# Attention's value product taken in blocks of three 512-query score chunks instead of one key tile

## The chip, the cores and the metric

The kernel runs on one core of one Trainium2 chip. The metric is the device time of one execution in microseconds (us); smaller is better.

## What is computed

The reference is one transformer block over two sequences of 2048 tokens with 256 channels: a layer norm with modulation, attention with 16 heads of 16 channels, a gated residual, and then a mixture of eight experts. Only the attention matters here; cut to it, for each of the 32 pairs of sequence and head:

```python
scores = jnp.einsum('bhqd,bhkd->bhqk', q, k) / jnp.sqrt(jnp.float32(Hd))   # 2048 x 2048 per head, Hd = 16
attn = jax.nn.softmax(scores, axis=-1)
out = jnp.einsum('bhqk,bhkd->bhqd', attn, v)
out = out.transpose(0, 2, 1, 3).reshape(B, T, D)
return out @ W_o + b_o
```

All operands are float32. The weights are scaled so that the scores are large, so the row maxima are subtracted before the exponential.

## The kernel before

The program is a row of stages: modulation and norm, projection of q, k and v, attention, output projection with the second norm, and the experts. The change touches attention (lines 487 to 766), and only the counts of some waits in the stage after it.

Attention works on 64 units. A unit is one head and one half of its queries (1024 queries, two chunks of 512), against 16 tiles of 128 keys; one unit is 16 steps, one per key tile, and there are 1024 steps. Each step has three kinds of TensorE work.

- `fill_group` (L724) computes scores with queries on the partitions, for 128 queries and 1024 keys, as two matmuls of 512 columns. The group lies in one of two slots of two PSUM banks. VectorE reduces it to row maxima (L695). This work is done 24 steps (`AHEAD`) before the step that needs the maxima. After a unit's 16 groups VectorE joins the maxima (L701) and turns them (L707); GpSimd splits them in two parts (L616, L618), and DMAs of SyncE's queue put them beside the q operand (L540, L545).
- `scores` (L737) computes the same scores with keys on the partitions, 128 keys by 512 queries, with the maxima subtracted by extra rows of the contraction. There is one matmul for each half of the queries; each fills one of three PSUM banks (`SCORE_BANKS`). Chunk n is half n % 2 of step n // 2. ScalarE turns each chunk into probabilities in `pt` (L677, the exponential), which has six slots of one step. Chunk n may be computed when the exponential of chunk n - 3 has ended.
- `weigh` (L749) multiplies the probabilities with the values and a column of ones. The 1024 queries are four strips of 256, each on its own 32 columns of the array and its own 32 partitions of bank 7. Operands are float32, and the program has two instructions for each call, so a step has eight weight loads and eight matmuls. I call the four that run side by side a stage: a step's `weigh` is two stages of 256 columns.

The array stands in two layouts. `fill_group` and `scores` contract over 48 and 50 rows, and use rows 0 to 63 for one half and rows 64 to 127 for the other: two such matmuls, one in each row half, can run together. I call such a pair, or a lone one, a slot. `weigh` uses all 128 rows and a quarter of the columns. So a step goes from one layout to the other and back once.

The order on TensorE is written out by hand. Step s runs `weigh(s - 3)`, `scores(s, 0)`, `fill_group(s + 24)`, `scores(s, 1)`; once in a unit, where a new unit's first tile is weighed, the first two change places, so that ScalarE has time to copy the finished unit out of bank 7 (`take_output`, L667). SyncE's queue stores this copy, loads it back turned to the layout of the output projection (L563) and loads the sums of the exponentials in four pieces (L569); later VectorE inverts the sums (L510), they go out and come back by DMA (L515, L518), and GpSimd normalises (L523).

Of the kernel before, what the change touches and what calls it, by code (L numbers as in the profile page):

```python
# [20 lines left out]
HD = D // H  # L21
# [27 lines left out]
QT = TH // P  # L49
LEAD = 8  # L50
AHEAD = KT + LEAD
LAG = 3
PTS = 6
HG = D // HD // KD
BITS = 7
# [27 lines left out]
def adaln_moe_block(nc, x, w_q, b_q, w_k, b_k, w_v, b_v, w_o, b_o, w_s, router_w, router_b,  # L83
                    w1, b1, w2, b2, c, w_mod, out):
    ctx = ExitStack()
    with ctx:
# [400 lines left out]
        with nc.Block() as block:  # L487
# [15 lines left out]

            acc = bank(7)[:, 0:STRIP]

            def group_slot(n):
                return bank(3 + 2 * (n % 2), 2)

# [17 lines left out]
            def _(sp):  # L526
# [30 lines left out]
                def load_output(u):  # L557
                    g, f = divmod(u, HALVES)
                    rows = slice((g % HG) * HD, (g % HG + 1) * HD)
                    cols = slice(f * TH, (f + 1) * TH)  # L560
                    strips = o_dram[u].rearrange("(j r) c -> r j c", r=32)
                    sp.wait_ge(o_stored[u % 2], (u // 2 + 1) * 16)
                    sp.dma_start(ao[rows, g // HG, cols].rearrange("r (j c) -> r j c", c=STRIP),  # L563
                                 strips[0:HD]).then_inc(o_in[f], 16)
                    if g >= HG:
                        sp.wait_ge(inverse_saved, ((g // HG - 1) * HALVES + f + 1) * 16)
                    for j in range(4):
                        at = (g % HG) * HD + 4 * j
                        sp.dma_start(sums_c[at:at + 4, f, :],  # L569
                                     strips[HD, j].rearrange("(q c) -> q c", q=4)).then_inc(sums_in[f], 16)  # L570

                def finish_group(u):
                    h, f = divmod(u, HALVES)
# [26 lines left out]
            def _(pool):  # L600
# [2 lines left out]
                                          v_all[:, (h // H) * KT:(h // H + 1) * KT, (h % H) * HD:(h % H + 1) * HD]).then_inc(v_staged, 1)  # L603

                def restage_v(h):
                    pool.wait_ge(pv_done, (h - NBUF + 1) * HALVES * KT)
                    stage_v(h, h % NBUF)

                g = nc.gpsimd
# [8 lines left out]
                    g.tensor_tensor(low, rowmax_t[:], high, ALU.subtract).then_inc(parts_made, 1)  # L618

                def normalise_part(k, f):  # L620
                    pool.wait_ge(o_in[f], (k + 1) * HG * 16)
                    pool.wait_ge(inverse_in[f], (k + 1) * HG * 16)
                    normalise(g, k, f).then_inc(normalised, 1)

# [36 lines left out]
            @block.scalar  # L661
            def _(act):
                def take_output(u):
                    act.wait_ge(pv_done, (u + 1) * KT)
                    if u > 1:
                        act.wait_ge(o_stored[u % 2], (u // 2) * 16)
                    nc.scalar.copy(o_sb[:, u % 2, :], acc).then_inc(acc_out, 1)  # L667

                for s in range(STEPS):
                    if s % KT == LAG - 1 and s > KT:  # L670
                        take_output(s // KT - 1)
                    if s >= PTS:
                        act.wait_ge(pv_done, s - PTS + 1)
                    for half in range(2):
                        n = s * 2 + half
                        act.wait_ge(scores_full, n + 1)
                        nc.scalar.activation(pt[:, s % PTS, half * CH:(half + 1) * CH], bank(n % SCORE_BANKS),  # L677
                                             ACT.Exp, scale=SCALE).then_inc(scores_out, 1)
                take_output(UNITS - 1)

            @block.vector
            def _(dve):
                v = nc.vector
                def invert(u):
                    h, f = divmod(u, HALVES)
                    dve.wait_ge(sums_in[f], (h + 1) * 64)
# [24 lines left out]
            def _(pe):  # L711
# [16 lines left out]
                def scores(s, half):  # L728
                    u, kt = divmod(s, KT)
                    h, f = divmod(u, HALVES)  # L730
                    n = s * 2 + half
# [8 lines left out]
                def weigh(s):  # L740
                    u, kt = divmod(s, KT)
                    h = u // HALVES
                    if kt == 0:
                        pe.wait_ge(v_staged, h + 1)
                        if u > 0:
                            pe.wait_ge(acc_out, u)
                    pe.wait_ge(scores_out, (s + 1) * 2)
                    for j in range(4):
                        last = mm(acc[32 * j:32 * (j + 1), :], v_st[:, h % NBUF, kt, :],  # L749
                                  pt[:, s % PTS, j * STRIP:(j + 1) * STRIP], start=kt == 0, stop=kt == KT - 1)  # L750
                    last.then_inc(pv_done, 1)

                for n in range(AHEAD):
                    fill_group(n)
                for s in range(STEPS):
                    first = (s - LAG) % KT == 0
                    if s >= LAG and not first:
                        weigh(s - LAG)
                    scores(s, 0)
                    if s >= LAG and first:  # L760
                        weigh(s - LAG)
                    if AHEAD + s < STEPS:
                        fill_group(AHEAD + s)
                    scores(s, 1)
                for s in range(STEPS - LAG, STEPS):
                    weigh(s)


        h2_t = pt[:, 1:4:2, :].rearrange("p s (k t) -> p s k t", k=KD)
# [17 lines left out]
        with nc.Block() as block:  # L787
# [21 lines left out]
            def _(pool):  # L809

                pool.sem_inc(xn2_read, 2)
                for n in range(chunks):
                    if n == 2:
                        pool.wait_ge(o_in[1], G * 16)
# [35 lines left out]
            def _(dve):  # L850
# [42 lines left out]
                dve.wait_ge(xb_ready, 2 * NB)  # L893
                for n in range(chunks):
                    if n == 2:
                        dve.wait_ge(sums_in[1], G * 64)
# [516 lines left out]
```

## Time and profile before

| | us |
|---|---|
| three runs | 1897.76, 1904.01, 1913.08; median 1904.01 |
| the profiled execution | 1902.33 |
| its span, first to last instruction | 1900.5 |
| attention with all three kinds of work, 200 to 1447 us of the span | 1247 |
| attention's last steps, without `fill_group` | 28 |

The profiled execution lies 1.7 us below the median of the runs, and its span 1.8 us below its own time. In the stretch of 1247 us the engines are busy for this long: TensorE 1247.0, VectorE 1215.1, ScalarE 1086.7. A matmul's recorded time includes its way through the array, and those of neighbours overlap, so a busy TensorE is not one that takes in a column in each cycle; distances between starts say more. The clock granted to TensorE is the full one (2.4 GHz) there.

### The profile page before, as it was taken

The numbers are of one execution on the slowest core, as the hardware profiler recorded it, in microseconds if no ns is written. First come the engines' busy times: TensorE is split into PE (matmuls) and PEld (weight loads), VectorE is DVE, ScalarE is ACT, GpSimd is POOL, SyncE is SP. The second block draws the span as 40 slices with busy tenths as digits, with TensorE's granted clock in tenths as the row PEclk, the third lists the DMA queues.
The fourth block names the chain that finished last, engine by engine and source line by source line (L and its number), as shares of the span: only waits on it lengthen the run. The fifth ranks groups of instructions, "written<-read, shape, count | busy, mean of one in ns | idle before, by whom it ended". The sixth has DMA issues, their size and how long they took to land. (4 is left out here: it accounts for less than half of the span.)

```text
span 1900.5 us, 36936 instructions
## 1 busy us (share of the span) xinstructions
PE 1742.6 (92%) x14142; PEld 780.6 (41%) x14142; DVE 1531.2 (81%) x1942; ACT 1221.6 (64%) x2266; POOL 244.1 (13%) x301
## 2 busy tenths in 40 slices
PE   5985999999999999999999999999999671599997
PEld 3652333333333333333333333333333560275665
DVE  4436899999999999999999999999994478544431
ACT  1330788888888888888888888888889110112121
POOL 2007100000010000001000000000000262232422
PEclk8995899999999999999999999999999775699999
DMA  5448132222332223222223222232200430034432
GB/s 178 176 185 155 24 46 38 38 36 46 54 61 38 36 37 56 43 45 54 36 47 52 38 38 47 49 56 43 37 14 12 161 133 0 22 87 113 98 101 23
DMA packets 87458, 121.32 MB, mean 64 GB/s; under 512 B 22592, under 2 KB 65152, under 8 KB 84096
## 3 DMA queue, kind: packets, MB, share of 16 engines
q1 hardware_dynamic: 78880, 109.12, 26.2%
q0 software_dynamic: 6144, 8.39, 2.7%
q8 instruction: 106, 1.74, 0.4%
q10 hardware_dynamic: 2272, 1.61, 0.3%
q14 instruction: 56, 0.46, 0.1%
HBM read 80.53 MB, written 38.54 MB: 63 GB/s over the span
## 5 line engine op out<-in xcount | busy, mean ns | idle before, releaser
L695 DVE TENSOR_REDUCE pmax<-ps 128x2 f32<-128x1024 f32 x1024 | 1230.4, 1220 | 53.4 <-PE ps L724 43.3
L677 ACT ACTIVATE pt<-ps 128x512 f32<-128x512 f32 x2048 | 1110.7, 596 | 212.5 <-PE ps L737 172.0
L724 PE MATMUL ps<-kp,qp 48*128 48x512 f32 x2048 | 736.0, 460 | 24.2 <-DMA kp<-k_parts 15.8
L737 PE MATMUL ps<-qp,kp 50*128 50x512 f32 x2048 | 753.3, 447 | 5.2 <-DMA qp<-m_rows 5.2
L749 PE MATMUL ps<-pt,v_st 128*32 128x256 f32 x8192 | 657.6, 393 | 0.0
L737 PEld LDWEIGHTS ps<-qp,kp 50*128 50x128 f32 x2048 | 315.6, 186 | 416.2 <-ACT pt L677 351.2
L724 PEld LDWEIGHTS ps<-kp,qp 48*128 48x128 f32 x2048 | 290.9, 188 | 62.7 <-issue 26.3
L749 PEld LDWEIGHTS ps<-pt,v_st 128*32 128x32 f32 x8192 | 161.5, 108 | 367.9 <-ACT pt L677 298.9
L1248 ACT ACTIVATE ao<-ps,b_col 128x512 f32<-128x512 f32 x64 | 44.0, 687 | 192.4 <-PE ps L1372 192.4
L616 POOL CAST m_parts<-rowmax_t 128x32 fp32r<-128x32 f32 x64 | 13.4, 209 | 853.1 <-DVE rowmax_t L707 853.1
L1372 PE MATMUL ps<-stage_b,v_all 128*128 128x512 f32 x256 | 119.1, 613 | 1.5 <-DVE stage_b L1264 1.5
L1386 PE MATMUL ps<-v_all,ao 128*128 128x256 f32 x512 | 112.5, 380 | 0.8 <-ACT ao L1248 0.8
L1386 PEld LDWEIGHTS ps<-v_all,ao 128*128 128x128 f32 x512 | 96.7, 190 | 14.6 <-ACT ao L1248 1.6
L1313 DVE TENSOR_TENSOR contrib<-ps,b_row 128x256 f32<-128x256 f32 x32 | 13.6, 425 | 82.6 <-PE ps L1386 82.6
L1372 PEld LDWEIGHTS ps<-stage_b,v_all 128*128 128x128 f32 x256 | 48.1, 194 | 54.6 <-issue 52.3
L602 POOL COPY v_st<-v_all 128x256 f32<-128x256 f32 x32 | 12.6, 396 | 438.4 <-PE ps L749 311.3
L1223 POOL DMA_INDIRECT y<-contrib,scatter_at x32 | 52.1, 1627 | 67.8 <-DVE contrib L1317 64.1
L1205 POOL DMA_INDIRECT stage_a<-h_rows,gather_at x32 | 32.9, 1028 | 161.6 <-DVE gather_at L1287 153.6
L1276 DVE TENSOR_TENSOR one_hot<-lane,col_row 128x1024 bf16<-128x1024 bf16 (+1 forms) x32 | 37.7, 1222 | 18.0 <-PE ps L1350 16.6
L928 PE MATMUL ps<-wog,ao 128*128 128x256 f32 x128 | 34.2, 429 | 14.1 <-DVEq L853 14.1
L1240 ACT COPY list_t<-ps 128x128 f32<-128x128 f32 x8 | 2.1, 259 | 66.7 <-PE ps L1350 66.7
L838 ACT ACTIVATE nwt<-nwt 128x4 f32<-128x4 f32 x8 | 1.6, 205 | 55.6 <-DVE nwt L874 55.6
(185 smaller groups left out, 813.1 us busy)
## 6 DMA issues: line engine op xcount, KB each, us to landing
kp<-k_parts SPq DMA_DIRECT2D x192, 128.0 KB, 4.7
v_all<-L_ffn_w SPq DMA_DIRECT2D x16, 1024.0 KB, 8.3
qp<-q_parts SPq DMA_DIRECT2D x192, 64.0 KB, 4.5
q_parts<-pt SPq DMA_DIRECT2D x16, 512.0 KB, 2.7
k_parts<-pt SPq DMA_DIRECT2D x16, 512.0 KB, 3.0
o_rows<-o_sb SPq DMA_DIRECT2D x64, 128.0 KB, 1.7
ao<-L_attn_x SPq DMA_DIRECT2D x2, 2048.0 KB, 18.4
xb<-L_attn_x SPq DMA_DIRECT2D x2, 2048.0 KB, 21.7
```

Of the source, the lines that this page charges most:

```text
L677: nc.scalar.activation(pt[:, s % PTS, half * CH:(half + 1) * CH], bank(n % SCORE_BANKS), ACT.Exp, scale=SCALE).then_inc(scores_out, 1)
L695: v.reduce_max(pmax[:, u % 2, 2 * k:2 * k + 2], group_slot(n).rearrange("p (f t) -> p f t", f=2), AX.X).then_inc(groups_out, 1)
L724: last = mm(group_slot(n)[:, half * CH:(half + 1) * CH], qp[rows, r, a * P:(a + 1) * P], kp[rows, r, c * CH:(c + 1) * CH], start=True, sto ...
L737: mm(bank(n % SCORE_BANKS), kp[rows, h % NBUF, kt * P:(kt + 1) * P], qp[rows, h % NBUF, f * CH:(f + 1) * CH], start=True, stop=True).then_ ...
L749: last = mm(acc[32 * j:32 * (j + 1), :], v_st[:, h % NBUF, kt, :], pt[:, s % PTS, j * STRIP:(j + 1) * STRIP], start=kt == 0, stop=kt == KT ...
L928: last = mm(bank(2 + half)[:, t * D:(t + 1) * D], ao[:, n // NCH * KD + k, at:at + P], wog[:, n // NCH, k, :], start=k == 0, stop=k == KD - 1)
L1205: nc.gpsimd.indirect_dma_start(tok_rows[:, par, cc, :], None, h2_dram, bass.IndirectOffsetOnAxis(ap=gather_at[:, par, cc:cc + 1], axis=0)) ...
L1223: nc.gpsimd.indirect_dma_start(out_flat, bass.IndirectOffsetOnAxis(ap=scatter_at[:, par, cc:cc + 1], axis=0), contrib[:, cc, :], None, com ...
L1248: nc.scalar.activation(hid[:, f, :], bank(2 + f % 2), ACT.Relu, bias=b1_col[:, bass.ds(e * NF + f, 1)]).then_inc(hid_out, 1)
L1276: v.tensor_tensor(one_hot[:, g8 % 2], lane[:, bass.ds(n, 1), g8 * 8:(g8 + 1) * 8].squeeze(1).unsqueeze(2).broadcast_to([P, 8, P]), col_row ...
L1372: last = mm(bank(2 + f % 2), w1_sb[par][:, k, f * P:(f + 1) * P], tok_t[:, par, k, :], start=k == 0, stop=k == KD - 1)
L1386: last = mm(bank(eo_banks[cc])[:, 0:D], hid[:, f, cc * P:(cc + 1) * P], w2_sb[par][:, f, :], start=f == 0, stop=f == NF - 1)
```

## The change

The value product is no longer taken once per key tile but once per block of three chunks. A unit's 32 chunks make eleven blocks: ten of three chunks, and a last one of two. A block of three holds one tile with both halves of the queries and one half of another tile. To make this possible, the strips of bank 7 are laid out anew: strip j holds 128 queries of the first half and 128 of the second, so that a half tile is a matmul of 128 columns for each strip, and a full tile one of 256. TensorE's order is now, for each block, `weigh` of the block two before it, and then the block's three chunks, with a `fill_group` ahead of each even chunk. The exchange at a unit's start is gone. ScalarE waits for a free slot of `pt` at each chunk, and copies out a unit after the third chunk of the next. With the new layout the turned output is loaded by two DMAs instead of one, and the sums by eight instead of four.

```diff
-LAG = 3
+BLOCK = 3
+DELAY = 2
+UNIT_CHUNKS = 2 * KT
+BLOCKS = -(-UNIT_CHUNKS // BLOCK)
+QB = CH // 4
...
+            def chunks_of(block):
+                u, b = divmod(block, BLOCKS)
+                return range(u * UNIT_CHUNKS + b * BLOCK, u * UNIT_CHUNKS + min((b + 1) * BLOCK, UNIT_CHUNKS))
...
-                    sp.dma_start(ao[rows, g // HG, cols].rearrange("r (j c) -> r j c", c=STRIP),
-                                 strips[0:HD]).then_inc(o_in[f], 16)
+                    for half in range(2):
+                        part = ao[rows, g // HG, f * TH + half * CH:f * TH + (half + 1) * CH]
+                        sp.dma_start(part.rearrange("r (j c) -> r j c", c=QB),
+                                     strips[0:HD, :, half * QB:(half + 1) * QB]).then_inc(o_in[f], 16)
...
-                        sp.dma_start(sums_c[at:at + 4, f, :],
-                                     strips[HD, j].rearrange("(q c) -> q c", q=4)).then_inc(sums_in[f], 16)
+                        for half in range(2):
+                            at = (g % HG) * HD + half * (HD // 2) + 2 * j
+                            sp.dma_start(sums_c[at:at + 2, f, :], ...
...
-                for s in range(STEPS):
-                    if s % KT == LAG - 1 and s > KT:
-                        take_output(s // KT - 1)
+                for n in range(STEPS * 2):
+                    if n % UNIT_CHUNKS == BLOCK and n > UNIT_CHUNKS:
+                        take_output(n // UNIT_CHUNKS - 1)
+                    s, half = divmod(n, 2)
                     if s >= PTS:
-                        act.wait_ge(pv_done, s - PTS + 1)
...
+                        act.wait_ge(pv_done, blocks_until(n - 2 * PTS))
+                    act.wait_ge(scores_full, n + 1)
...
-                    pe.wait_ge(scores_out, (s + 1) * 2)
-                    for j in range(4):
-                        last = mm(acc[32 * j:32 * (j + 1), :], v_st[:, h % NBUF, kt, :],
-                                  pt[:, s % PTS, j * STRIP:(j + 1) * STRIP], start=kt == 0, stop=kt == KT - 1)
+                    ready = chunks_of(block)
+                    pe.wait_ge(scores_out, ready[-1] + 1)
+                    for s in sorted({n // 2 for n in ready}):
+                        kt = s % KT
+                        halves = [n % 2 for n in ready if n // 2 == s]
+                        first, many = halves[0], len(halves)
+                        probs = pt[:, s % PTS, first * CH:(first + many) * CH].rearrange("p (h t) -> p h t", h=many)
+                        for j in range(4):
+                            last = mm(acc[32 * j:32 * (j + 1), first * QB:(first + many) * QB], v_st[:, h % NBUF, kt, :],
+                                      probs[:, :, j * QB:(j + 1) * QB], start=kt == 0, stop=kt == KT - 1)
...
-                for s in range(STEPS):
-                    first = (s - LAG) % KT == 0
-                    if s >= LAG and not first:
-                        weigh(s - LAG)
-                    scores(s, 0)
-                    if s >= LAG and first:
-                        weigh(s - LAG)
-                    if AHEAD + s < STEPS:
-                        fill_group(AHEAD + s)
-                    scores(s, 1)
+                blocks = UNITS * BLOCKS
+                for block in range(blocks):
+                    if block >= DELAY:
+                        weigh(block - DELAY)
+                    for n in chunks_of(block):
+                        if n % 2 == 0 and AHEAD + n // 2 < STEPS:
+                            fill_group(AHEAD + n // 2)
+                        scores(n)
+                for block in range(blocks - DELAY, blocks):
+                    weigh(block)
```

## Rows read from the trace of the kernel before

**Rows 1.** The page: busy time of each engine, share of the span.

```profile
PE 1742.6 (92%) x14142; PEld 780.6 (41%) x14142; DVE 1531.2 (81%) x1942; ACT 1221.6 (64%) x2266; POOL 244.1 (13%) x301
```

**Rows 2.** Busy time by stretch: PE, PEld, DVE, ACT, POOL, PEclk, DMA share, GB/s.

```profile
200.00:1447.00 1247.00, 1247.00 (x11906) 468.14 (x11902) 1215.09 (x1121) 1086.68 (x2046) 54.49 (x159) 1.00 0.26 42
1447.00:1475.00 28.00, 27.90 (x256) 10.69 (x254) 1.36 (x4) 25.34 (x51) 0.46 (x2) 1.00 0.04 12
```

**Rows 3.** Groups by line and shape, 300 to 1450 us: busy, mean ns, idle before.

```profile
L695 DVE TENSOR_REDUCE pmax<-ps 128x2 f32<-128x1024 f32 x914 | 1099.3, 1220 | 23.8 <-PE ps L724 14.5
L737 PEld LDWEIGHTS ps<-qp,kp 50*128 50x128 f32 x1833 | 281.0, 185 | 365.2 <-ACT pt L677 314.9 <-issue 50.2
L749 PE MATMUL ps<-pt,v_st 128*32 128x256 f32 x7336 | 586.0, 391 | 0.0
L749 PEld LDWEIGHTS ps<-pt,v_st 128*32 128x32 f32 x7328 | 144.1, 108 | 329.4 <-ACT pt L677 272.7 <-issue 56.6
```

**Rows 4.** Timeline of one step: start us, length us, engine, line, count.

```profile
431.88 0.50 PE L737 MATMUL ps<-qp,kp 50*128 50x512 f32 x1
431.89 0.73 PE L724 MATMUL ps<-kp,qp 48*128 48x512 f32 x2
432.23 0.40 PE L737 MATMUL ps<-qp,kp 50*128 50x512 f32 x1
432.48 1.09 ACT L677 ACTIVATE pt<-ps 128x512 f32<-128x512 f32 x2
432.56 0.64 PE L749 MATMUL ps<-pt,v_st 128*32 128x256 f32 x8
432.80 0.40 PE L749 MATMUL ps<-pt,v_st 128*32 128x256 f32 x4
433.13 0.50 PE L737 MATMUL ps<-qp,kp 50*128 50x512 f32 x1
```

**Rows 5.** Timeline of the step in which a unit's first tile is weighed.

```profile
434.37 0.50 PE L737 MATMUL ps<-qp,kp 50*128 50x512 f32 x1
434.71 0.64 PE L737 MATMUL ps<-qp,kp 50*128 50x512 f32 x2
```

**Rows 6.** Timeline of VectorE where a unit's maxima end.

```profile
422.99 0.21 DVE L707 STREAM_TRANSPOSE rowmax_t<-rowmax 128x32 f32<-128x32 f32 x1
440.35 2.46 DVE L695 TENSOR_REDUCE pmax<-ps 128x2 f32<-128x1024 f32 x2
443.07 0.21 DVE L707 STREAM_TRANSPOSE rowmax_t<-rowmax 128x32 f32<-128x32 f32 x1
443.20 1.18 DVE L695 TENSOR_REDUCE pmax<-ps 128x2 f32<-128x1024 f32 x1
443.20 2.31 DVE L695 TENSOR_REDUCE pmax<-ps 128x2 f32<-128x1024 f32 x2
```

**Rows 7.** Timeline of attention's last steps, without fill_group.

```profile
1469.30 0.49 PE L737 MATMUL ps<-qp,kp 50*128 50x512 f32 x2
1469.88 0.60 ACT L677 ACTIVATE pt<-ps 128x512 f32<-128x512 f32 x1
1470.53 0.50 PE L737 MATMUL ps<-qp,kp 50*128 50x512 f32 x1
1470.96 0.42 PE L749 MATMUL ps<-pt,v_st 128*32 128x256 f32 x4
1471.53 0.50 PE L737 MATMUL ps<-qp,kp 50*128 50x512 f32 x2
1473.43 0.61 PE L749 MATMUL ps<-pt,v_st 128*32 128x256 f32 x8
```

**Rows 8.** Timeline of SyncE's queue behind the last unit.

```profile
1477.43 1.33 SPq L569 DMA_DIRECT2D sums_c<-o_rows  x4
1480.33 3.54 SPq L518 DMA_DIRECT2D stage_a<-inverse_sums  x8
```

**Rows 9.** Timeline of eight turned 128x128 tiles in the experts.

```profile
1662.96 1.09 PE L1337 MATMUL ps<-ident,stage_a 128*128 128x128 f32 x8
```

More of the change, by code:

```diff
@@ L504, in adaln_moe_block, with blocks_until @@
             acc = bank(7)[:, 0:STRIP]
+            def blocks_until(n):
+                return n // UNIT_CHUNKS * BLOCKS + n % UNIT_CHUNKS // BLOCK + 1
+            def chunks_of(block):
+                u, b = divmod(block, BLOCKS)
+                return range(u * UNIT_CHUNKS + b * BLOCK, u * UNIT_CHUNKS + min((b + 1) * BLOCK, UNIT_CHUNKS))
             def group_slot(n):
@@ L559, in load_output @@
                     rows = slice((g % HG) * HD, (g % HG + 1) * HD)
-                    cols = slice(f * TH, (f + 1) * TH)
                     strips = o_dram[u].rearrange("(j r) c -> r j c", r=32)
                     sp.wait_ge(o_stored[u % 2], (u // 2 + 1) * 16)
-                    sp.dma_start(ao[rows, g // HG, cols].rearrange("r (j c) -> r j c", c=STRIP),
-                                 strips[0:HD]).then_inc(o_in[f], 16)
+                    for half in range(2):
+                        part = ao[rows, g // HG, f * TH + half * CH:f * TH + (half + 1) * CH]
+                        sp.dma_start(part.rearrange("r (j c) -> r j c", c=QB),
+                                     strips[0:HD, :, half * QB:(half + 1) * QB]).then_inc(o_in[f], 16)
                     if g >= HG:
@@ L567, in load_output @@
                     for j in range(4):
-                        at = (g % HG) * HD + 4 * j
-                        sp.dma_start(sums_c[at:at + 4, f, :],
-                                     strips[HD, j].rearrange("(q c) -> q c", q=4)).then_inc(sums_in[f], 16)
+                        for half in range(2):
+                            at = (g % HG) * HD + half * (HD // 2) + 2 * j
+                            sp.dma_start(sums_c[at:at + 2, f, :],
+                                         strips[HD, j, half * QB:(half + 1) * QB].rearrange("(q c) -> q c", q=2)
+                                         ).then_inc(sums_in[f], 16)
                 def finish_group(u):
@@ L605, in restage_v @@
                 def restage_v(h):
-                    pool.wait_ge(pv_done, (h - NBUF + 1) * HALVES * KT)
+                    pool.wait_ge(pv_done, (h - NBUF + 1) * HALVES * BLOCKS)
                     stage_v(h, h % NBUF)
@@ L620, in normalise_part @@
                 def normalise_part(k, f):
-                    pool.wait_ge(o_in[f], (k + 1) * HG * 16)
+                    pool.wait_ge(o_in[f], (k + 1) * HG * 32)
                     pool.wait_ge(inverse_in[f], (k + 1) * HG * 16)
@@ L663, in take_output @@
                 def take_output(u):
-                    act.wait_ge(pv_done, (u + 1) * KT)
+                    act.wait_ge(pv_done, (u + 1) * BLOCKS)
                     if u > 1:
@@ L667, in take_output @@
                     nc.scalar.copy(o_sb[:, u % 2, :], acc).then_inc(acc_out, 1)
-                for s in range(STEPS):
-                    if s % KT == LAG - 1 and s > KT:
-                        take_output(s // KT - 1)
+                for n in range(STEPS * 2):
+                    if n % UNIT_CHUNKS == BLOCK and n > UNIT_CHUNKS:
+                        take_output(n // UNIT_CHUNKS - 1)
+                    s, half = divmod(n, 2)
                     if s >= PTS:
-                        act.wait_ge(pv_done, s - PTS + 1)
[L674 to L678, printed above, removed]
+                        act.wait_ge(pv_done, blocks_until(n - 2 * PTS))
+                    act.wait_ge(scores_full, n + 1)
+                    nc.scalar.activation(pt[:, s % PTS, half * CH:(half + 1) * CH], bank(n % SCORE_BANKS),
+                                         ACT.Exp, scale=SCALE).then_inc(scores_out, 1)
                 take_output(UNITS - 1)
@@ L685, in invert @@
                     h, f = divmod(u, HALVES)
-                    dve.wait_ge(sums_in[f], (h + 1) * 64)
+                    dve.wait_ge(sums_in[f], (h + 1) * 128)
                     inverse(v, f).then_inc(inverse_made, 1)
@@ L726, in fill_group, with scores @@
                     last.then_inc(groups_full, 1)
-                def scores(s, half):
+                def scores(n):
+                    s, half = divmod(n, 2)
                     u, kt = divmod(s, KT)
                     h, f = divmod(u, HALVES)
-                    n = s * 2 + half
                     if kt == 0 and half == 0:
@@ L738, in scores, with weigh @@
                        qp[rows, h % NBUF, f * CH:(f + 1) * CH], start=True, stop=True).then_inc(scores_full, 1)
-                def weigh(s):
-                    u, kt = divmod(s, KT)
+                def weigh(block):
+                    u, b = divmod(block, BLOCKS)
                     h = u // HALVES
-                    if kt == 0:
+                    if b == 0:
                         pe.wait_ge(v_staged, h + 1)
@@ L754, in _ @@
                     fill_group(n)
-                for s in range(STEPS):
-                    first = (s - LAG) % KT == 0
-                    if s >= LAG and not first:
-                        weigh(s - LAG)
-                    scores(s, 0)
-                    if s >= LAG and first:
-                        weigh(s - LAG)
-                    if AHEAD + s < STEPS:
-                        fill_group(AHEAD + s)
-                    scores(s, 1)
-                for s in range(STEPS - LAG, STEPS):
-                    weigh(s)
+                blocks = UNITS * BLOCKS
[8 more added lines that the diff above has]
+                    weigh(block)
         h2_t = pt[:, 1:4:2, :].rearrange("p s (k t) -> p s k t", k=KD)
@@ L813, in _ @@
                     if n == 2:
-                        pool.wait_ge(o_in[1], G * 16)
+                        pool.wait_ge(o_in[1], G * 32)
                         pool.wait_ge(inverse_in[1], G * 16)
@@ L895, in _ @@
                     if n == 2:
-                        dve.wait_ge(sums_in[1], G * 64)
+                        dve.wait_ge(sums_in[1], G * 128)
                         inverse(v, 1).then_inc(inverse_made, 1)
```

## The prediction

> **What bounds the kernel now.** I read the page first [rows 1]: TensorE is busy for 92% of the span, VectorE for 81%. The table by stretch [rows 2] says that attention takes 1247 us of 1900.5, and that VectorE is busy there for 1215.1 us, 97%. That looks like a kernel bound by VectorE, and the groups [rows 3] seem to agree, with 23.8 us of idle time before 914 reductions. The timeline says otherwise. Right behind a unit's end two reductions take 2.31 us and the first of them 1.18, so the next starts 1.13 us later [rows 6]: that is VectorE's pace when its slots are full. In the steady steps it starts one per 1.24 us, since it waits for a group that TensorE ends just then: the busy time hides the overlap of neighbours. A unit's floor on VectorE is 15 x 1.13 + 1.61 = 18.56 us, where 1.61 runs from the start of the last reduction (440.35 + 2.46 - 1.22 = 441.59) to 443.20 [rows 3, 6]. A unit takes 443.07 - 422.99 = 20.08 us. ScalarE's pace is 1.09 - 0.60 = 0.49 us a chunk [rows 4, 7], 32 x 0.49 + the copy, some 16 us. So TensorE sets the pace.
>
> The groups put 587 us of idle weight loads down to ScalarE [rows 3]. I don't take that as a wait: the exponentials that `weigh` and the next `scores` need ended more than half a microsecond earlier, as the order in the code and the starts in [rows 4] show. These are in-order weight loads behind a change of layout.
>
> The pieces of a step are in [rows 4]. First slot to second 0.35, second slot to `weigh` 0.33, first stage of `weigh` to its second 0.24, second stage to the next step 0.33. The last digits are rounded; with 0.34 for the first piece a step is 1.24 (431.88 to 433.13 rounds to 1.25). A slot in the middle, between two others, costs 0.64 - 0.40 = 0.24 [rows 5]. 16 x 1.24 + 0.24 = 20.08 gives the measured unit. Within one layout stages follow at 0.61 - 0.38 - 0.02 = 0.21 to 0.22 [rows 7]; 256 columns therefore stream in 0.21, and so do 512 columns of one slot. A change of layout and back thus costs about 0.34 + 0.33 + 0.24 + 0.33 - 4 x 0.215 = 0.38 us over bare streaming.
>
> **The change part by part.**
>
> *Fewer changes of layout, other slots.* Three steps were three visits to `weigh`; now they are two. An even block (A) runs fill pair, score pair, fill pair, lone score: four slots, 0.34 + 0.24 + 0.24 + 0.33 = 1.15. An odd block (B) runs score with fill, fill with score, lone score: three slots, 0.34 + 0.24 + 0.33 = 0.91. The last block (C) has two slots, 0.67. So per unit 37 slots take the place of 33 (32 and the lone one of [rows 5]): the chunks no longer pair as well, and this gives back 4 x 0.24 of the gain.
>
> *`weigh` of a block.* It has 16 matmuls: two stages of 256 columns and two of 128, where three tiles had six stages of 256. The streamed columns are the same, but the weights of the split tile are loaded twice. No row shows a stage of 128 columns. Its streaming is half of 0.215, 0.107; its four weight loads of 108 ns run side by side [rows 3]. Bounds: 0.109 (the pace of loads with 128 columns streamed, (1.09 - 0.33) / 7 [rows 9], 0.33 being the length of the first of these, and the others at even distances) and 0.136, when the load starts behind the four starts of the stage before (0.027 + 0.109). I take 0.12. Then `weigh` is 0.24 + 0.22 + 0.12 + (0.33 - 0.11) = 0.80, in either order of the stages; for block C it stays 0.57. The Trainium skill (TensorE: Matmul & The Clock Gate, LDWEIGHTS) has the load take the column count divided by 1.2 GHz, 27 ns for 32 columns. The trace doesn't agree for float32: 108 ns [rows 3]. By the page a short stage would be at its streaming time, and `weigh` 0.79.
>
> *Sum if TensorE alone decided:* 5 x 1.15 + 5 x 0.91 + 0.67 + 10 x 0.80 + 0.57 = 19.54 us a unit, 0.54 under 20.08.
>
> *The wait for ScalarE.* With three banks, the third chunk of B needs the exponential of the third chunk of A. From A's start: chunks 0 and 1 start at 0.34 and end at 0.74; the exponential starts 0.10 later, as 432.48 against 431.88 + 0.50 [rows 4], and three at 0.49 put the third at 1.82, with its end at 2.42. A waiting score starts 0.05 behind the exponential (1469.88 + 0.60 to 1470.53) and `weigh` 0.43 behind that (1470.96) [rows 7]: 2.90, where slots alone say 1.15 + 0.80 + 0.91 = 2.86. So A and B together take 2.90 + 0.80 = 3.70 and not 3.66. At a unit's start, where the short `weigh` of 0.57 stands between A and B, the same chain holds 3.70. This wait also makes the price of the middle slots irrelevant. The other scores wait for exponentials that end 0.06 us or more before their loads. The copy of a unit (L667) starts at the third chunk's end, and has room under B's slots; nothing waits for it.
>
> *The wait for VectorE.* Two fills of A lie 0.58 apart, and a slot of banks is free only when the reduction two groups back has ended. In the steady pairs VectorE needs 3 x 1.13 = 3.39 of 3.70, and both fills find their slot free by about 0.1 us. At a unit's end the maxima take 1.61 instead of 1.13. The last group is filled by block 4, the next unit's first by block 5. The chain: reductions at 0.55 and 1.68 of block 4, the next at 3.29, which ends at 4.47; the second fill of block 6 wants its slot at 3.70 + 0.58 = 4.28 and gets it at 4.52. That is 0.24 late, of which 0.04 comes back, since block 7 then doesn't wait for ScalarE: 0.20 a unit.
>
> *A unit:* 5 x 3.70 + 0.20 + C with one `weigh` (0.67 + 0.80) = 20.17 us against 20.08. [Rows 2] hold 62 units (992 reductions in 1247 us): +0.09 x 62 = +6 us.
>
> *Attention's last 24 steps.* Now 2.23 us for two (1469.30 to 1471.53) [rows 7], 26.8 for all. After: 16 blocks without fills, each held by its own third chunk: exponentials at 0.59, 1.08, 1.57 from the block's start (0.49 + 0.10), the last ending at 2.17; score at 2.22, `weigh` at 2.65, its end at 3.45 is two blocks on. 1.725 x 16 = 27.6: +0.8.
>
> *DMAs.* `load_output` issues five more, at 1.33 / 4 = 0.33 us each [rows 8]. In the middle SyncE's queue has room: it issues 12 or 24 DMAs in 20 us, and the maxima's DMAs stand ahead of these. After the last unit they stand ahead of the ones for the inverse sums, for which the normalisation and then the next stage wait: 5 x 0.33 = +1.7. If the normalisation were hidden there, 0.
>
> *Waits of ScalarE* per chunk instead of per step: an instruction each, hidden by the exponential that runs before it; without that cover 0.06 x 1024 would be 61 us, but only the first of a block finds ScalarE idle, and I have counted 0.10 for it.
>
> Sum: 6 + 0.8 + 1.7 = +8.5 us on the profiled execution's 1902.3, which is 1910.8; I predict 1911. The median of the runs lies 1.7 above that execution, which is nothing at this scale. About 1% (19 us) is what a measurement of this kernel can tell from no change.
>
> **The rivals.**
>
> *TensorE alone decides (faster).* If the wait for ScalarE or for VectorE gives way (the third score's load runs ahead, or a reduction frees its slot earlier), a unit is 19.54: -0.54 x 62 = -33, with +2.5 behind it 1871; with middle slots at 0.22 and nothing in the way 19.2, 1850. For it: the waits are 0.04 and 0.24 long, shorter than some roundings that I added up. Against: both chains are built from pieces seen waiting.
>
> *A short stage costs more than its columns (slower).* The place is the 128-column stages of `weigh`, 20 a unit. If such a stage costs as much as one of 256, 0.22, then `weigh` is 1.01 and the loss 0.21 x 10 x 62 = +130, 2040; halfway, 0.17, it is +62, 1973. It decides from 0.135 a stage, where ten `weigh` a unit give 10 more us to the sum of 8.5. For it: loads of 108 ns are as long as the streaming they should hide under, and this is close to the upper bound above. Against: [rows 9].
>
> *TensorE's instruction supply (slower).* Three steps had 36 matmuls with as many loads in 3.72 us, 103 ns a pair. Now there are 44 in 3.70, 84 ns. A pair costs at most that 103 and at least nothing that shows. If 103 were the floor, three steps would take 4.54, +280 us; at 87 it would be 3.83, +43, 1954. It decides from 86. Against: the extra slot of [rows 5] lengthened the step by its 0.24 at an equal number of instructions, so supply was not the limit at 103; and [rows 7] run eight matmuls inside 0.24 us from the queue. The skill (same page, "Wait — 56ns, not 53.3ns?") knows a decoding in which each matmul costs about 62 ns. By it 44 matmuls need 2.7 us of 3.70, and nothing changes; no run here shows which decoding is on.
>
> *The change doesn't do what it says:* the 0.33 ahead of `weigh` is no price of the layout, so fewer visits save nothing. Then only the extra slots and stages stay, 5 x 0.3 + 8 more, +90 us. Against: 0.24 and 0.22 within a layout and 0.33 at each change [rows 4, 5, 7].
>
> **How the numbers follow.** Forecast 0.43, with its own range 1890 to 1925 (short stage 0.109 to 0.136, -7 to +10; the two waits and the roundings, some 10 either way). TensorE alone 0.26. Short stage 0.16. Instruction supply and no saving 0.15 together. To leave out no more than a tenth on each side, the range runs from 1864, inside the faster rival, to 1975, about the middle of the short-stage rival. Faster by over 1% (under 1885): 0.26 and 0.02 of the forecast, 0.28. Slower by over 1% (over 1923): 0.31 and 0.04 of the forecast, less a little of the rivals' mild ends, 0.33. Within: 0.39.
>
> **What would show it.** A: four slots of 1.15 between two `weigh`; `weigh` 0.80 long, with stages 0.24, 0.22 and 0.12 apart; a pair of blocks 3.70; the third score of B starting 0.05 behind an exponential's end; one late fill a unit, in the third pair; VectorE at 1.13 in most reductions, with idle time in front of one in three. I am wrong if the short stages stand over 0.136 apart, if the lone score of A or B pairs with something, if fills find no slot in the steady pairs, or if loads come in even distances with no wait ahead of them.

## The result and the profile after

The changed kernel takes 1944.29 us (median of four runs, 1912.35 to 1950.35) against 1901.49 for the kernel before in the same comparison, so the medians stand at 1.0225. The forecast was 1911 and no change; the range held the time.

The ratio of the comparison is smaller, 1.0121 with a 95% interval of 1.0062 to 1.018, because it leaves out runs that lie over 1.5% above the fastest, and here these belong to what the change does. So below I give all runs, with the granted clock as a mean over the run. The four runs of this comparison and the six of the next, all of the changed kernel, in order of time:

```
us      1907.1 1910.7 1912.4 1938.3 1938.4 1938.8 1950.3 1950.4 1951.2 1954.6
clock    0.941  0.939  0.937  0.924  0.924  0.924  0.917  0.916  0.916  0.913
```

The profiled execution is one of 1950.35 us, 48.0 above the one before, with a span of 1948.6. The page's busy times, and TensorE's granted clock in tenths over 40 slices of the span, answer to [rows 1]:

```profile
PE 1780.7 (91%) x16702; PEld 968.1 (50%) x16702; DVE 1499.6 (77%) x1942; ACT 1190.1 (61%) x2266; POOL 243.9 (13%) x301
PEclk8995557999999999999999999999999785599999
```

The clock's row of the page before:

```profile
PEclk8995899999999999999999999999999775699999
```

After the change the clock stays at five tenths into the seventh slice, where before it was up in the fifth; the steps of attention begin in the fourth. The table by stretch (PE, PEld, DVE, ACT, POOL busy, granted clock, DMA share, GB/s) puts numbers to that. First the kernel after, cut where the steps begin, where the clock rises, and where the steps end:

```profile
181.00:318.00 137.00, 137.00 (x924) 66.42 (x921) 77.52 (x72) 68.55 (x132) 11.66 (x12) 0.50 0.10 17
318.00:1518.00 1200.00, 1192.89 (x13819) 607.62 (x13820) 1115.65 (x1061) 1016.85 (x1973) 52.62 (x152) 1.00 0.26 43
```

Then the kernel before, over the same 137 us:

```profile
181.00:203.00 22.00, 19.25 (x100) 7.57 (x104) 11.51 (x12) 10.33 (x20) 13.46 (x5) 0.50 0.01 2
203.00:318.00 115.00, 115.00 (x1102) 43.02 (x1096) 111.78 (x102) 99.94 (x189) 3.51 (x13) 1.00 0.25 39
```

Look at the last column but two, 0.50 and 1.00, and at the count of VectorE's instructions: 72 in 137 us after, 114 before. TensorE's busy share is 1.00 at half clock, so it tells nothing of this. VectorE turns the maxima (STREAM_TRANSPOSE) once a unit, so the distance of two turns is the length of a unit. Here are two turns at half clock and then two at full clock:

```profile
229.26 0.21 DVE L720 STREAM_TRANSPOSE rowmax_t<-rowmax 128x32 f32<-128x32 f32 x1
263.69 0.21 DVE L720 STREAM_TRANSPOSE rowmax_t<-rowmax 128x32 f32<-128x32 f32 x1
...
810.38 0.21 DVE L720 STREAM_TRANSPOSE rowmax_t<-rowmax 128x32 f32<-128x32 f32 x1
...
830.52 0.21 DVE L720 STREAM_TRANSPOSE rowmax_t<-rowmax 128x32 f32<-128x32 f32 x1
```

A unit takes 34.43 us at 1.2 GHz (263.69 - 229.26). At 2.4 GHz it takes 20.14 here and 20.12 in the median, against 20.08 before [rows 6]. A microsecond at half clock thus costs 1 - 20.12 / 34.43 = 0.42 us. The kernel before costs the same at half clock: reductions start 2.17 us apart there (191.88, 194.05, 196.22), 34.7 for 16. The longer stretch at half clock (180.3 to 318.1 us after, 183.7 to 203.4 before) thus costs (137.8 - 19.7) x 0.42 = 50 us, about all of the 48. The 5 us added up further below come on top, and the steps began 3.4 us earlier in this execution; some 3 us between the sum and the 48 are not accounted for.

At full clock the blocks look as forecast. The timeline of TensorE over one pair answers to [rows 4]; the last two lines are cut from inside the `weigh` of 804.70, its first stage alone, and its second and third:

```profile
803.57 0.50 PE L737 MATMUL ps<-kp,qp 48*128 48x512 f32 x2
803.90 0.39 PE L750 MATMUL ps<-qp,kp 50*128 50x512 f32 x2
804.14 0.40 PE L737 MATMUL ps<-kp,qp 48*128 48x512 f32 x2
804.37 0.40 PE L750 MATMUL ps<-qp,kp 50*128 50x512 f32 x1
804.70 0.86 PE L768 MATMUL ps<-pt,v_st 128*32 128x128 f32 x16
805.49 0.49 PE L750 MATMUL ps<-qp,kp 50*128 50x512 f32 x1
805.49 0.73 PE L737 MATMUL ps<-kp,qp 48*128 48x512 f32 x2
805.83 0.68 PE L750 MATMUL ps<-qp,kp 50*128 50x512 f32 x2
806.44 0.86 PE L768 MATMUL ps<-pt,v_st 128*32 128x256 f32 x16
807.23 0.49 PE L737 MATMUL ps<-kp,qp 48*128 48x512 f32 x2
...
804.70 0.32 PE L768 MATMUL ps<-pt,v_st 128*32 128x128 f32 x4
...
804.84 0.51 PE L768 MATMUL ps<-pt,v_st 128*32 128x128 f32 x8
```

Block A is 804.70 - 803.57 = 1.13, `weigh` 0.79, B 0.95, the pair 3.66. The view names a group by its first shape: of the eight matmuls of the last line, four have 128 columns and four 256. The second stage starts 0.13 to 0.14 behind the first, and the third 0.51 - 0.38 - 0.02 = 0.11 behind that, 0.38 being the length of its matmuls of 256 columns: a short stage costs about its columns (half of 0.215). The weight loads under it are as long, 109 ns below, so which of the two sets the 0.11 isn't shown.

The groups by shape, 400 to 1450 us, answer to [rows 3]. The mean of 109 ns for a weight load is nearly that of before, and VectorE's idle time is twice what it was:

```profile
L708 DVE TENSOR_REDUCE pmax<-ps 128x2 f32<-128x1024 f32 x836 | 977.3, 1216 | 51.2 <-PE ps L737 50.0
...
L768 PE MATMUL ps<-pt,v_st 128*32 128x256 f32 x4592 | 360.5, 386 | 0.0
...
L768 PEld LDWEIGHTS ps<-pt,v_st 128*32 128x32 f32 x8768 | 215.2, 109 | 228.3 <-issue 145.6 <-ACT pt L690 37.9
```

The third score of B waits for ScalarE, as forecast. Its weight load starts 0.05 behind the end of A's third exponential (805.97 and 806.02; the view rounds start and length):

```profile
805.36 0.60 ACT L690 ACTIVATE pt<-ps 128x512 f32<-128x512 f32 x1
806.02 0.18 PEld L750 LDWEIGHTS ps<-qp,kp 50*128 50x128 f32 x1 [0.23 <-ACT pt L690]
```

The wait for VectorE at a unit's end is seen on both engines. VectorE's timeline answers to [rows 6], with TensorE's beneath it:

```profile
807.77 2.36 DVE L708 TENSOR_REDUCE pmax<-ps 128x2 f32<-128x1024 f32 x2 [0.17 <-PE ps L737]
810.16 0.19 DVE L714 TENSOR_REDUCE rowmax<-pmax 128x8 f32<-128x32 f32 x1
810.38 0.21 DVE L720 STREAM_TRANSPOSE rowmax_t<-rowmax 128x32 f32<-128x32 f32 x1
810.51 3.45 DVE L708 TENSOR_REDUCE pmax<-ps 128x2 f32<-128x1024 f32 x3
```

```profile
810.90 0.50 PE L737 MATMUL ps<-kp,qp 48*128 48x512 f32 x2
811.24 0.39 PE L750 MATMUL ps<-qp,kp 50*128 50x512 f32 x2
811.75 0.50 PE L737 MATMUL ps<-kp,qp 48*128 48x512 f32 x2
812.09 0.40 PE L750 MATMUL ps<-qp,kp 50*128 50x512 f32 x1
812.42 0.32 PE L768 MATMUL ps<-pt,v_st 128*32 128x128 f32 x4
```

The second pair of fills stands 0.51 behind the scores (811.24 to 811.75) and not 0.24, and its own first slot is a long one again (0.34). This block is 1.52 long, against 1.13 in the steady pairs. The pair is only 0.34 longer in the end, since B behind it no longer waits for ScalarE.

SyncE's queue behind the last unit answers to [rows 8]:

```profile
1523.21 0.34 SPq L566 DMA_DIRECT2D o_rows<-o_sb  x1
1524.90 0.78 SPq L575 DMA_DIRECT2D ao<-o_rows  x2
1525.72 2.35 SPq L582 DMA_DIRECT2D sums_c<-o_rows  x8
1528.18 0.34 SPq L526 DMA_DIRECT2D inverse_sums<-sums_c  x1
```

The first and the last of these in the kernel before:

```profile
1475.36 0.34 SPq L555 DMA_DIRECT2D o_rows<-o_sb  x1
1478.86 0.34 SPq L515 DMA_DIRECT2D inverse_sums<-sums_c  x1
```

From the store of the output to that of the inverse sums it is 4.97 us; before it was 3.50.

### The profile page after: what moved, and what is told of

Same layout as the page of the kernel before. It is cut to its first block and busy times, and to the rows that moved or that the text cites. A ratio compares the mean times of both kernels' runs of the same rounds, so it can differ in the third digit from the quotient of the medians.

```text
span 1948.6 us, 43394 instructions
## 1 busy us (share of the span) xinstructions
PE 1780.7 (91%) x16702; PEld 968.1 (50%) x16702; DVE 1499.6 (77%) x1942; ACT 1190.1 (61%) x2266; POOL 243.9 (13%) x301
## 5 line engine op out<-in xcount | busy, mean ns | idle before, releaser
L708 DVE TENSOR_REDUCE pmax<-ps 128x2 f32<-128x1024 f32 x1024 | 1198.1, 1216 | 135.8 <-PE ps L737 134.5
L690 ACT ACTIVATE pt<-ps 128x512 f32<-128x512 f32 x2048 | 1080.7, 602 | 294.4 <-PE ps L750 275.6
L750 PE MATMUL ps<-qp,kp 50*128 50x512 f32 x2048 | 642.3, 436 | 4.1 <-DMA qp<-m_rows 4.1
L768 PE MATMUL ps<-pt,v_st 128*32 128x256 f32 (+1 forms) x10752 | 616.9, 347 | 0.4 <-ACT pt L690 0.4
L737 PE MATMUL ps<-kp,qp 48*128 48x512 f32 x2048 | 578.1, 479 | 31.6 <-DMA kp<-k_parts 15.7
L768 PEld LDWEIGHTS ps<-pt,v_st 128*32 128x32 f32 x10752 | 271.9, 112 | 299.9 <-issue 181.2
L750 PEld LDWEIGHTS ps<-qp,kp 50*128 50x128 f32 x2048 | 303.9, 194 | 220.4 <-ACT pt L690 206.0
L737 PEld LDWEIGHTS ps<-kp,qp 48*128 48x128 f32 x2048 | 229.4, 194 | 186.5 <-issue 89.5
L945 PEld LDWEIGHTS ps<-wog,ao 128*128 128x128 f32 x128 | 27.2, 218 | 20.1 <-DVEq L870 15.9
```

Of the source, the lines that this page charges most:

```text
L737: last = mm(group_slot(n)[:, half * CH:(half + 1) * CH], qp[rows, r, a * P:(a + 1) * P], kp[rows, r, c * CH:(c + 1) * CH], start=True, sto ...
L768: last = mm(acc[32 * j:32 * (j + 1), first * QB:(first + many) * QB], v_st[:, h % NBUF, kt, :], probs[:, :, j * QB:(j + 1) * QB], start=kt ...
L945: last = mm(bank(2 + half)[:, t * D:(t + 1) * D], ao[:, n // NCH * KD + k, at:at + P], wog[:, n // NCH, k, :], start=k == 0, stop=k == KD - 1)
```

## The experiments

Theory 1: in steady state the change costs next to nothing, and the loss is a longer stretch at half clock at attention's start. Theory 2, the rival: the steady steps are slower by 1 to 2%, and the clock only differs by chance. The changed kernel was run again first.

> The changed kernel itself once more. Theory 1 (clock): its warm unit costs 20.12 us against 20.08 and the rest of the loss is the stretch at attention's start in which TensorE's clock stays at half speed (136 us in the profile after, 21 us before); that stretch should vary from run to run, with each microsecond of it worth 0.42 us, so times from about 1905 to 1950 that fall in line with the mean clock of the run. Theory 2 (steady cost): every run is longer by the same 1 to 2%, whatever its mean clock.

Six runs, 1907.05 to 1954.63, in the table above (1.0154 by the comparison's rule, 1.009 to 1.0219). Its profiled execution took 1907.05 us. The same stretch of it, by window:

```profile
181.00:211.00 30.00, 30.00 (x209) 14.71 (x211) 17.18 (x17) 14.74 (x29) 8.60 (x4) 0.50 0.01 2
211.00:318.00 107.00, 106.39 (x1235) 54.27 (x1225) 100.52 (x96) 90.26 (x177) 3.52 (x13) 1.00 0.26 42
```

The clock was at half for 180.9 us up to its rise in the run of 1950.35, and for 75.1 in this one: 105.8 x 0.42 = 44 us, and the runs differ by 43.3. Their units at full clock are the same to 0.01. Theory 2 has nothing left to explain between these two. All ten times fall in line with the mean clock. I call a run long when it is over 1920: seven of ten are. The kernel before has long runs too, up to 1960.72, but only 13 of the 88 that were taken here.

**The clock taken away.** In both kernels TensorE waits before and between the first groups of scores. These waits were filled with matmuls that nobody reads, into a score bank that is still free:

```diff
...
+                def warm(count):
+                    for _ in range(count):
+                        mm(bank(0)[:, 0:2 * P], ident_bf[:], ident[:].bitcast(BF16), start=True, stop=True)
+                warm(40)
                 for n in range(AHEAD):
                     fill_group(n)
+                    warm(2)
+                warm(20)
```

> The changed kernel with extra bf16 matmuls, whose results nobody reads, before attention's first group of scores, between the 24 groups that are made ahead, and before the first chunk. Theory 1: the clock is full when the steps begin, and the time is about 1892 to 1902 in every run, 1950 - 0.42 x 136 = 1893 and a few us for the extra work. Theory 2: it stays at 1930 or above.

> The kernel before with the same extra matmuls. Theory 1: 1902 - 0.42 x 21 = 1893, and at most 1% from the changed kernel with them, by my count 2.5 us for the units, 2 for the DMAs and 1 for the last steps faster. Theory 2: faster than the changed kernel with them by over 20 us.

The changed kernel: 1895.92 us, ten runs between 1895.29 and 1899.97 (0.9971 of the kernel before, 0.9948 to 0.9995). The kernel before: 1893.51, ten runs between 1891.58 and 1896.23 (0.9961, 0.9947 to 0.9975). The clock rises at 182 us of the span in both profiles and stays up. The spread of 47 us is gone, and the two kernels lie 2.4 us apart, as theory 1 has it: all but these 2.4 us of the loss is the clock. The table of the changed kernel:

```profile
137.00:182.00 45.00, 39.63 (x153) 17.18 (x151) 29.49 (x26) 0.76 (x1) 30.55 (x22) 0.58 0.92 173
182.00:318.00 136.00, 134.92 (x1557) 68.89 (x1557) 128.36 (x122) 114.20 (x222) 13.45 (x19) 1.00 0.24 37
```

**A burst alone.** Only the last 20 of these matmuls were kept.

> The changed kernel with only the last 20 of the extra matmuls, between the last group made ahead and the first chunk, while TensorE waits for the maxima anyway. If a short burst is enough for the clock, 1895 to 1900; if the clock needs the activity before it too, the spread of the changed kernel, 1907 to 1955.

Ten runs, 1894.21 to 1938.99, median 1911.06. In the profiled run (1912.93) the clock rose at 183.0 us, fell back at 186.4, and rose for good at 217.2. The table of three stretches of it:

```profile
181.00:186.00 5.00, 3.67 (x19) 2.02 (x18) 1.81 (x2) 0.84 (x2) 5.00 (x3) 0.80 0.02 6
187.00:216.00 29.00, 29.00 (x201) 13.94 (x205) 15.92 (x16) 13.82 (x27) 8.22 (x4) 0.50 0.01 2
218.00:318.00 100.00, 99.39 (x1160) 50.59 (x1158) 94.80 (x90) 84.74 (x165) 3.10 (x12) 1.00 0.22 36
```

So a rise just ahead of the steps isn't enough. Nine of the ten runs lie in the range of the second case, 1907 to 1955, in its lower part (three are long), and one at 1894 as the first case had it. The same burst in the kernel before wasn't run, so whether a step of the old order would have kept this clock is open.

**Blocks of two.** Is it the blocks of three that hold the clock low, or the rest of the change, or chance? Here the new layout of bank 7 and the new DMAs stay.

```diff
-BLOCK = 3
-DELAY = 2
+BLOCK = 2
+DELAY = 3
...
-                    if n % UNIT_CHUNKS == BLOCK and n > UNIT_CHUNKS:
+                    if n % UNIT_CHUNKS == 4 and n > UNIT_CHUNKS:
```

> The changed kernel with blocks of two chunks, one key tile, taken three blocks late, and the unit copied out after the fourth chunk: the new layout of bank 7 and the new DMAs are kept, the short stages and the joint visit are undone. At the full clock a unit should cost 16 x 1.24 = 19.84 us and some wait for the copy, near 20.1. Theory 1a (blocks of three keep the clock low): the stretch at half speed is as short as before, 1895 to 1915. Theory 1b (chance, or the rest of the change): it is long in some runs as in the changed kernel, up to 1950.

Eight runs, 1903.92 to 1913.73, median 1909.43 (1.0046, 1.003 to 1.0063). A unit takes 20.21 us at full clock, more than my 20.1. None of the runs is long, where on the same chip the changed kernel had four long ones of six. To keep blocks of three in steady state, the next kernel has blocks of two in the first four units only; a list of blocks takes the place of the arithmetic in `blocks_until`, `chunks_of` and the waits:

```diff
...
+TWOS = 4
+BLOCK_LIST = []
+for _u in range(UNITS):
+    _size = 2 if _u < TWOS else BLOCK
+    for _c in range(0, UNIT_CHUNKS, _size):
+        BLOCK_LIST.append(range(_u * UNIT_CHUNKS + _c, _u * UNIT_CHUNKS + min(_c + _size, UNIT_CHUNKS)))
```

> The changed kernel with its first four units (some 80 us at the full clock) in blocks of two chunks and all later ones in blocks of three; everything else as in the change. Theory 1a (blocks of three, as long as the clock is at half speed, keep it there, and don't bring it down once it is up): the half-speed stretch is short in nearly every run, 1898 to 1912 us, and later units cost 20.12 as in the change. Theory 1b (chance, the layout or the DMAs): a good part of the runs between 1930 and 1955 as in the changed kernel, seven of ten there.

Twelve runs, 1900.95 to 1914.00, median 1906.17 (1.0021, 0.9999 to 1.0042). The clock rises at 197.3 us in the profiled one, in the first unit, and the blocks of three behind it run at full clock with 20.12 a unit. With 7 of 10 long runs in the changed kernel, none of 8 and none of 12 can hardly be chance, though these twelve were taken on another chip. The kernel before, with 13 long runs of 88, might well give none of 12, so blocks of two are not shown to do better than it. Theory 1a holds as far as this goes: blocks of three delay the rise when they are what runs at half clock, and do not bring down a clock that has been full for some units. Behind the burst of 20 matmuls it had been full for 3.4 us only, and fell. What in them does it isn't settled. Filling the empty half of the lone slots was considered and not tried, since no bank is free for it.

**The wait for VectorE.** In each even block the second group was put behind the third score; the extra matmuls stayed, so that the clock plays no part.

```diff
...
                     for n in ready:
-                        if n % 2 == 0 and AHEAD + n // 2 < STEPS:
+                        late = len(ready) == 3 and n == ready[-1]
+                        if not late and n % 2 == 0 and AHEAD + n // 2 < STEPS:
                             fill_group(AHEAD + n // 2)
                         scores(n)
+                        if late and n % 2 == 0 and AHEAD + n // 2 < STEPS:
+                            fill_group(AHEAD + n // 2)
```

> The changed kernel with the extra matmuls ahead, and in each even block the second group of scores made behind the third chunk instead of ahead of it. By my slots it costs nothing in the steady pairs (the half of the group in the other rows runs beside the lone score), and it asks for its slot of banks 0.24 us later, so most of the wait for VectorE of 0.34 us a unit (measured in the profile after, 0.24 forecast) goes: a unit of 19.85 to 19.9 against 20.12, 12 to 16 us, 1880 to 1884. Rival: the group ends later, VectorE starts later by as much, and with 3.39 of 3.66 us busy it has no room to catch up; then 1896 or more.

1883.65 us, four runs between 1882.15 and 1885.44: 0.9865 of the kernel before (0.9794 to 0.9935), and 12.3 below the same kernel with the early fill. The timeline of TensorE in its block at a unit's end, and two turns of the maxima on VectorE:

```profile
811.80 0.50 PE L737 MATMUL ps<-kp,qp 48*128 48x512 f32 x2
812.14 0.68 PE L750 MATMUL ps<-qp,kp 50*128 50x512 f32 x3
812.64 0.50 PE L737 MATMUL ps<-kp,qp 48*128 48x512 f32 x2
813.07 0.86 PE L768 MATMUL ps<-pt,v_st 128*32 128x128 f32 x16
...
811.27 0.21 DVE L720 STREAM_TRANSPOSE rowmax_t<-rowmax 128x32 f32<-128x32 f32 x1
...
831.17 0.21 DVE L720 STREAM_TRANSPOSE rowmax_t<-rowmax 128x32 f32<-128x32 f32 x1
```

The three scores run through, and the block is 1.27 long (811.80 to 813.07) where it was 1.52. A unit is 19.90, as expected.

**The wait for ScalarE.** On top of that, the two scores of an even block were put ahead of its first group:

```diff
...
+                    if ready[0] % 2 == 0:
+                        scores(ready[0])
+                        scores(ready[1])
+                        fill(ready[0])
+                        if len(ready) == 3:
+                            scores(ready[2])
+                            fill(ready[2])
...
```

> As the late fill with the extra matmuls ahead, and in each even block (the short last one too) the two scores now stand ahead of the first group. Their exponentials end 0.25 us earlier, so the third score of the odd block no longer waits for ScalarE. Theory: that wait is 0.05 us a pair (odd block 0.95 measured against 0.91 for its slots), so a unit falls from 19.90 to 19.6 or 19.7, 12 to 18 us in all, about 1868. Rival: the groups end 0.25 us later, and VectorE (floor 18.56 us a unit) or the free slot becomes the wait instead; then 19.9 or more a unit.

1895.93 us, ten runs (0.9974, 0.9952 to 0.9996): my expectation failed and its rival held. A unit is 20.10 again (816.53 to 836.69 in one, 20.16). VectorE now waits for a group again and again, and the groups for a slot of banks. The idle time that their weight loads spend on VectorE shows it, over 400 to 1430 us; the first line is of the kernel with the late fill:

```profile
L737 PEld LDWEIGHTS ps<-kp,qp 48*128 48x128 f32 x1650 | 197.4, 184 | 79.8 <-issue 72.6 <-DVE pmax L708 0.6
...
L737 PEld LDWEIGHTS ps<-kp,qp 48*128 48x128 f32 x1640 | 179.7, 185 | 40.1 <-DVE pmax L708 30.8
```

And VectorE's own waits:

```profile
805.20 1.23 DVE L708 TENSOR_REDUCE pmax<-ps 128x2 f32<-128x1024 f32 x1 [0.19 <-PE ps L737]
806.66 2.35 DVE L708 TENSOR_REDUCE pmax<-ps 128x2 f32<-128x1024 f32 x2 [0.24 <-PE ps L737]
```

That is not all of it. The wait for ScalarE has gone from the third score of B, whose load now starts 0.16 us or more behind the exponential in four of a unit's five B blocks, but it has come up in A: the load of A's second score starts 0.05 behind one (824.46 to 824.52), and so does that of the third. How the 0.2 us a unit divide between the two waits isn't shown.

**The late fill without extra matmuls**, alone and behind four units in blocks of two:

> The late fill in the changed kernel without extra matmuls. Its unit at the full clock is 19.90 us, so with a half-speed stretch as short as before it comes to 1892 to 1898. If the stretch depends on where the second group stands in the even blocks, it is short in most runs. If it comes from blocks of three as such (the long visits to the value product, the lone scores), the stretch is long in over half of the runs and these take 1920 to 1942, as 7 of 10 of the changed kernel took 1938 to 1955.

> The first four units in blocks of two, the later ones in blocks of three with the late fill, no extra matmuls. The clock should rise within the first two units as it did in all runs with blocks of two there, and the later units cost 19.90 instead of 20.12: 1906 - 0.22 x 58 = 1893, in every run within 1888 to 1902. Rival: blocks of three with the late fill hold a clock that is up less well, and some runs lie over 1910.

Alone: twelve runs, 1895.13 to 1940.44, median 1909.95 (1.0014, 0.9973 to 1.0055). Four are over 1920, a smaller share than in the changed kernel, and about that of the kernel before beside them (7 of 23); neither of my two cases. But this kernel starts from a unit that is 0.22 shorter, so the count makes it look too well. Its median lies 26 us above the same kernel with the extra matmuls; for the kernel before that distance is 10, for the changed kernel 43 over its ten runs. So its stretch at half clock is longer than before and shorter than in the changed kernel. Behind blocks of two: twelve runs, 1888.43 to 1897.86, median 1894.95 (0.9945, 0.992 to 0.997), as forecast, and 11 above the kernel with the extra matmuls. The fastest version found is the late fill with the extra matmuls, 1883.65.

## Why the prediction was right or wrong

- *TensorE sets the pace, not VectorE or ScalarE.* Right. The change moved the starts of its slots and stages to where the sum had them.
- *Slots.* A 1.13 against 1.15; 37 slots a unit, the lone ones alone.
- *`weigh` of a block.* 0.79 against 0.80, the short stages 0.13 and 0.11 against 0.12. The rival of a dear short stage is refuted, and that of the instruction supply too: 44 matmuls and their loads go in 3.66 us, 83 ns a pair, where it would have decided from 86.
- *The wait for ScalarE.* B is 0.95 and its slots 0.91, as 2.90 against 2.86 had it. That it is ScalarE is read from the trace, where the load starts 0.05 behind the exponential in four of a unit's five B blocks, and 0.24 behind it in the one that follows the late group, which by the forecast no longer waits. The experiment that should have removed the wait brought up others instead, so the 0.04 stand as a reading and not as a test.
- *The wait for VectorE at a unit's end.* Right in its place, the third pair, and too small: 0.34 a unit against 0.20. I forgot that a group which waits also starts with a long first slot (0.34 for 0.24). The late fill made the unit 0.22 shorter, which shows the cause.
- *A unit* 20.12 against 20.17, so +2.5 us for 62 units in place of +5.6. The last steps, from the last turn of the maxima to the end of the last `weigh`: 28.2 (1494.54 to 1522.74) against 27.2 (1447.66 to 1474.90), +1.0 for +0.8. The DMAs: +1.5 up to the store of the inverse sums, for +1.7. Together +5, for +8.5. The pair of kernels with extra matmuls measured +2.4, half of that. Part of the difference is the unit: in the profiles of that pair the first and last turns of the maxima, 63 units apart, grew by 1.4 us only (169.39 to 1439.98 against 169.95 to 1439.16).
- *What failed* is a term that the sum didn't have. The prediction took "the clock granted to TensorE is the full one there" for the whole stretch of 1247 us, and the same stretch at 0.50 ahead of it as given. The page before showed the half clock at attention's start, and [rows 2] begins just where it ends. When it rises depends on what runs, and with blocks of three that was 33 and 138 us behind the first score in two profiles, where it was 20 in that of the kernel before. No rival named it. The range held the time by luck: it was wide for other reasons, a dear short stage and the instruction supply, neither of which exists. The chance of 0.33 for slower by over 1% stood on the same two. The range of the likeliest case, 1890 to 1925, holds three of the ten runs.

## What to carry to other kernels

Where a long dense stage begins at half clock, the time at which the clock rises is a term of its own: read the granted clock in windows at the stage's start in both traces, and give every run's mean clock beside its time before comparing medians. Matmuls whose results nobody reads, put into waits that TensorE has anyway ahead of the stage, made two kernels faster and cut their spread from 47 and 65 us to 5. To judge a regrouping of work on one engine, count slots and changes of layout, and then walk each chain over the other engines' buffers once, at the unit's end too; moving one group by one slot in each even block was worth 12.3 us, five times what the whole regrouping cost at full clock.

## What the runs showed of the hardware

- TensorE stood at 1.2 GHz for 137 us while the trace has it busy for all of them, with 924 matmuls. The Trainium skill (TensorE: Matmul & The Clock Gate, Loop structure matters more than you think) says that matmuls back to back keep the clock up. That agrees with what follows the rise here, 1200 us at 1.00. It doesn't explain the stretch ahead of it.
- A full clock was lost again 3.4 us after it came (183.0 to 186.4 us) when the blocks of three began behind the burst of 20 matmuls, and kept from 182 us on when the extra work reached further back.
- Back to back, VectorE's reductions of 1024 columns recorded as 1.22 us start every 1.13 us, and ScalarE's exponentials recorded as 0.60 every 0.49 [rows 4, 6].
- A stage of four matmuls of 128 float32 columns on four column quarters costs 0.11 us, as long as the weight loads of 109 ns under it; 0.13 to 0.14 as the first stage of a `weigh`.
